# Probabilities transposed in 32x32 squares on VectorE and carried by DMA, in an f32 graph-attention layer

## The reference

```
q, k, v = heads(x @ Wq + bq), heads(x @ Wk + bk), heads(x @ Wv + bv)
scores = einsum('bhqd,bhkd->bhqk', q, k) / sqrt(64)
probs = softmax(scores + where(adj, 0, -9e15)[:, None])
ctx = einsum('bhqk,bhkd->bhqd', probs, v)
out = layernorm(x + merge(ctx) @ Wf + bf)
```

## Time and profile before

| | |
|---|---|
| median of 3 runs | 1510.48 us (1510.31 to 1511.2) |
| the profiled execution | 1509.4 us, its span 1507.4 us |
| PE busy | 1471.1 us, 98% |
| PE's weight loads | 1141.7 us, 76% |
| DVE, ACT, POOL busy | 898.2, 873.4, 378.2 us |
| TensorE's granted clock | 0.997 of full |
| DMA | 51.41 MB, mean 34 GB/s |

### The profile page before, as it was taken

The page is one execution under the profiler, slowest core; times in us unless marked ns, Lnnn a source line. Parts: engine busy times, 40 slices in busy tenths (PEclk is TensorE's granted clock), DMA queues, the critical chain, the costliest instruction groups (busy, mean ns, idle before and its releaser), DMA issues.

```text
span 1507.4 us, 32054 instructions
## 1 busy us (share of the span) xinstructions
PE 1471.1 (98%) x11088; PEld 1141.7 (76%) x11088; DVE 898.2 (60%) x1769; ACT 873.4 (58%) x1637; POOL 378.2 (25%) x676
## 2 busy tenths in 40 slices
PE   7999999999999999999999999999999999999996
PEld 6777787777877778777787777877778777787764
DVE  5666645665556655666555665566655666465654
ACT  4566626666266662666636665366654666546662
POOL 2112242122411224122141221412214122141222
PEclk9999999999999999999999999999999999999998
DMA  3110101100011000100001100011001110000000
GB/s 129 36 40 30 29 27 38 38 29 29 27 50 29 29 29 24 50 30 29 30 24 50 40 29 20 29 49 35 29 19 37 50 29 30 15 25 19 30 22 28
DMA packets 47925, 51.41 MB, mean 34 GB/s; under 512 B 9089, under 2 KB 47745, under 8 KB 47745
## 3 DMA queue, kind: packets, MB, share of 16 engines
q1 hardware_dynamic: 47744, 49.12, 10.5%
HBM read 36.31 MB, written 12.78 MB: 33 GB/s over the span
## 4 chain that ended last, share of the span: by engine, by line
PE 92%; DVE 3%; issue 2%; ACT 1%; POOL 1%; DMA 0%; DVEq 0%; SPq 0%; ACTq 0%; POOLq 0%
PE turn_ps L457 23%; PE context_ps L470 22%; PE score_ps L444 20%; PE misc_ps L356 4%; PE misc_ps L355 4%; PE misc_ps L354 4%; PE score_ps L354 3%; PE score_ps L355 3%; PE score_ps L356 3%; DVE prob L660 1%; PE context_ps L354 1%; PE turn_ps L354 1%; PE context_ps L356 1%; PE context_ps L355 1%; PE misc_ps L362 1%
## 5 line engine op out<-in xcount | busy, mean ns | idle before, releaser
L660 DVE CUSTOM_DVE_ANT_0 prob<-score_ps,mask 128x1024 f32<-128x1024 f32 x384 | 455.0, 1222 | 252.5 <-PE score_ps L444 232.7
L568 ACT ACTIVATE prob_t<-turn_ps 128x512 f32<-128x512 f32 x384 | 229.5, 598 | 431.6 <-PE turn_ps L457 431.6
L559 ACT ACTIVATE prob<-prob,row_min 128x1024 f32<-128x1024 f32 x384 | 442.1, 1151 | 64.3 <-DVE row_min L660 64.3
L457 PE MATMUL turn_ps<-ident,prob 128*128 128x128 f32 x3072 | 413.1, 276 | 9.8 <-ACT prob_t L568 5.5
L457 PEld LDWEIGHTS turn_ps<-ident,prob 128*128 128x128 f32 x3072 | 337.7, 140 | 94.8 <-issue 78.0
L470 PE MATMUL context_ps<-prob_t,v_all 128*64 128x256 f32 x3072 | 372.1, 385 | 0.8 <-ACT prob_t L568 0.8
L470 PEld LDWEIGHTS context_ps<-prob_t,v_all 128*64 128x64 f32 x3072 | 204.6, 136 | 148.9 <-issue 64.0
L806 POOL TENSOR_TENSOR context_lo<-context,context_hi 128x256 fp32r<-128x256 f32 x96 | 70.6, 735 | 938.6 <-ACT context_hi L582 938.6
L669 DVE COPY prob_t<-turn_ps 128x512 f32<-128x512 f32 x192 | 131.7, 686 | 30.7 <-PE turn_ps L457 30.2
L444 PE MATMUL score_ps<-k_hi,q_hi 64*128 64x512 f32 x768 | 140.9, 444 | 4.8 <-issue 3.8
L444 PE MATMUL score_ps<-k_lo,q_hi 64*128 64x512 f32 x768 | 120.4, 390 | 0.0
(11 more groups left out here) (85 smaller groups left out, 1834.9 us busy)
## 6 DMA issues: line engine op xcount, KB each, us to landing
x_in<-in_x_dram SPq DMA_DIRECT2D x32, 384.0 KB, 3.4
inv_rows<-spread_dram SPq DMA_DIRECT2D x192, 64.0 KB, 2.6
out_dram<-res SPq DMA_DIRECT2D x32, 384.0 KB, 2.5
adj_in<-in_adj_dram SPq DMA_DIRECT2D x64, 128.0 KB, 2.2
spread_dram<-inv_turned SPq DMA_DIRECT2D x384, 0.5 KB
prob_t<-in_L_gnn_Wk_dram SPq DMA_DIRECT2D x1, 576.0 KB, 4.3
prob_t<-in_L_gnn_Wq_dram SPq DMA_DIRECT2D x1, 576.0 KB, 7.1
prob_t<-in_L_gnn_Wv_dram SPq DMA_DIRECT2D x1, 576.0 KB, 8.3
```

The source lines that it names most:

```text
L457: last = pe.transpose(turn_ps[:, half, i, :], prob[:, u % 4, kt * P:(kt + 1) * P], ident[:])
L559: nc.scalar.activation(prob[:, t % 4, :], prob[:, t % 4, :], ACT.Exp, scale=-1.0, bias=row_min[:, t % 4:t % 4 + 1], accum_out=row_sum[:, t ...
L568: nc.scalar.activation(prob_t[:, pair % 2, head, 0:4, qt * P:(qt + 1) * P], turn_ps[:, 0], ACT.Copy).then_inc(copied[0], 1)
L660: nc.vector.tensor_tensor_reduce(prob[:, t % 4, :], score_ps[:, t % 2, :], mask[:, qt, :], 1.0, HUGE, ALU.add, ALU.min, row_min[:, t % 4:t ...
```

## The change

PE's transposes, their PSUM tile `turn_ps` and the copies out of it are gone. In their place DVE transposes each 32x32 square of a unit where it stands (`turn_squares`), and sixteen DMAs a slot carry the squares to the partitions of their keys (`move_square`): source partitions 32a to 32a+31, both heads, keys 256c to 256c+255, to the partitions 32c to 32c+31 of `prob_t`. One such DMA has 64 rows of 1 KB. Those with a+c odd are issued from SP's queue, those with a+c even from ACT's. To make a block of 32 partitions hold the keys that it gets, x^T is stored with its tokens permuted (`tokens`).

More changes with it. The layout of inverted row sums is no round trip through DRAM any more: POOL makes a diagonal (`make_diagonal`), and PE multiplies it with ones (job i, 12 a batch). The lo halves of x, k and q are made on POOL from a second copy that ACT makes (`raw`), where DVE made them from PSUM. ACT also copies v out; its bias is folded into the output bias. The whole group is mixed at once (job m), one slot or more after its second slot. `prob` has three slots where it had two. The table `STEADY` says which jobs PE does in which slot; the batch is written out three times (first, the loop of six, last).

```diff
+    9: [("i", 3, 0, 0), ("m", 3, 0, 0)],
+    10: [("x", 0, 0, 1), ("x", 1, 0, 1), ("x", 2, 0, 1), ("q", 0, 2, 0), ("p", 0, 0, 0)],
...
-        prob = sb("prob", [P, 4, S], F32)
-        prob_t = sb("prob_t", [P, 2, 2, TT, GQ], F32)
+        prob = sb("prob", [P, 2 * RING, S], F32)
+        prob_t = sb("prob_t", [P, 2, 2, 2, 4, GQ], F32)
...
+        def move_square(queue, s, a, c):
+
+            group, qt, ring = s // 2, s % 2, s % RING
+            queue.dma_start(prob_t[32 * c:32 * c + 32, group % 2, :, qt, a, :],
+                            prob[32 * a:32 * a + 32, 2 * ring:2 * ring + 2, GQ * c:GQ * c + GQ]
+                            ).then_inc(landed[ring], 16)
...
-                        last = pe.transpose(turn_ps[:, half, i, :], prob[:, u % 4, kt * P:(kt + 1) * P], ident[:])
...
+            def mix(b, group):
+                pe.wait_ge(context_done, at(b, GROUPS, group + 2))
+                for s in (2 * group, 2 * group + 1):
+                    pe.wait_ge(landed[s % RING], at(b, 256 * SLOTS // RING, 256 * (s // RING + 2)))
...
+            def move(b, s):
+                act.wait_ge(squared, at(b, UNITS, 2 * s + 2))
+                if s % 2 == 0:
+                    act.wait_ge(mixed, at(b, GROUPS, s // 2 + 1))
+                for a in range(4):
+                    for c in range(4):
+                        if (a + c) % 2 == 0:
+                            move_square(act, s, a, c)
+
+            def body(b):
+                for s in slots_of(b.mode):
+                    work = slot_work(b.mode, s)
+                    if s < SLOTS:
+                        exponential(b, 2 * s)
+                        exponential(b, 2 * s + 1)
+                    for job in work:
+                        if job[0] not in "pm":
+                            evict(b, job)
+                    if s < SLOTS:
+                        move(b, s)
+                    for job in work:
+                        if job[0] == "m":
+                            context_high(b, job[1])
...
+            def turn_squares(b, t):
+                ring = 2 * (t // 2 % RING) + t % 2
+                dve.wait_ge(exp_done, at(b, UNITS, t + 1))
+                dve.sem_inc(dve_waited, 1)
+                nc.vector.transpose(prob[:, ring, :], prob[:, ring, :]).then_inc(squared, 1)
...
+                    if s < SLOTS:
+                        mask_scores(b, 2 * s)
+                        mask_scores(b, 2 * s + 1)
+                        turn_squares(b, 2 * s)
+                        turn_squares(b, 2 * s + 1)
```

More of the change, by code:

```diff
@@ L72 @@
[L72 to L78, removed]
@@ L81, in mid_job @@
[L81 to L100, removed]
+SLOTS = 24
+RING = 3
+STEADY = {
[24 rows of a table added]
+}
+FIRST_0 = [("k", 1, 0, 0), ("k", 1, 1, 0), ("q", 1, 0, 0)]
@@ new lines, with slot_work @@
+X_LOADS = {1: (0, 0), 2: (0, 1), 3: (0, 2), 4: (0, 3), 11: (1, 0), 12: (1, 1), 13: (1, 2), 14: (1, 3)}
+RESIDUALS = {1: 0, 2: 1, 11: 2, 17: 3}
+NORMALISE = {3: -2, 10: -1, 13: 0, 18: 1}
+START_STEPS = ([("weight", 1)] + [("job", job) for job in START_JOBS[:6]] + [("weight", 0)]
+               + [("job", START_JOBS[6]), ("weight", 2), ("job", START_JOBS[7]), ("weight", 3), ("job", START_JOBS[8])])
+@dataclass(frozen=True)
+class Batch:
+    mode: str
+    it: Any
+    off: int
+def slot_work(mode, s):
+    if s >= SLOTS:
+        return LAST_24 if mode == "last" else []
+    if mode == "first" and s < 2:
+        return FIRST_0 if s == 0 else FIRST_1
+    if mode == "last" and s == 22:
+        return LAST_22
+    return [w for w in STEADY[s] if not (mode == "first" and w[1] < 0) and not (mode == "last" and w[3] == 1)]
@@ L103, in graph_attention, with slots_of @@
+def slots_of(mode):
+    return range(SLOTS + 1 if mode == "last" else SLOTS)
+MODES = ("first", "mid", "last")
+JOBS = {mode: [w for s in slots_of(mode) for w in slot_work(mode, s) if w[0] != "m"] for mode in MODES}
+EVICTED = {mode: [w for w in JOBS[mode] if w[0] != "p"] for mode in MODES}
+SPLITS = {mode: [w for w in EVICTED[mode] if w[0] not in "vi"] for mode in MODES}
 def graph_attention(nc, x, adj, wq, bq, wk, bk, wv, bv, wf, bf, out):
@@ new lines, in _ @@
+            pe.wait_ge(weights_done, 4)
+            pe.wait_ge(bv_wide_done, 1)
+            for t in range(FT):
+                last = pe.matmul(job_ps[:, 0, 0:H], bv_wide[:, t, :], weight_raw[:, 3, t, :],
+                                 start=(t == 0), stop=(t == FT - 1))
+            last.then_inc(bv_mixed, 1)
+            pe.wait_ge(ones_done, 1)
+            body(Batch("first", 0, 0))
+            with pe.Fori(0, len(loop)) as it:
+                body(Batch("mid", it, 1))
+            body(Batch("last", 0, BATCH - 1))
@@ L612, in _, with start_high @@
-            for kind, what in start_steps():
+            def start_high(job):
+                act.wait_ge(job_done, START_JOBS.index(job) + 1)
+                bank = job_bank("start", job)
+                if job[0] == "x":
+                    half = slice(512 * job[2], 512 * job[2] + 512)
+                    nc.scalar.activation(tokens(xt_hi, job[1], half), as_tokens(bank), ACT.Copy).then_inc(hi_done, 1)
+                else:
+                    width, hi, _ = job_parts(job)
+                    bank = bank[:, 0:width]
+                    which = 1 if job[0] == "k" else 0
+                    nc.scalar.activation(hi, bank, ACT.Identity,
+                                         bias=bias_qk[:, which, job[1]:job[1] + 1]).then_inc(hi_done, 1)
@@ L613, in _ @@
+            for kind, what in START_STEPS:
                 if kind == "weight":
```

878 lines of the change are left out of this document (420 added, 458 removed), and 22 rows, old and new, of the table STEADY.

## The result

The changed kernel takes **2015.56 us** (median of 4 runs, 2014.09 to 2016.73); beside it the kernel before took 1510.76 us. The ratio is 1.334, with an interval of 1.332 to 1.336. The forecast was 1676 us, 11% slower. The direction was right and the size was far off: 33% slower, near the upper end of the range. The profiled execution has a span of 2014.0 us and a mean granted clock of 0.834.

The account below looks back on a forecast made before the run. PE bound the kernel before; ACT's issue ring would bound the changed one. 22 to first masking + 5 + 1476 for 191 periods of 7.73 + 143 extras + 26.5 tail = 1673 us span, forecast 1676, range 1490 to 2100.

Parts of the forecast that it names:

- The ring: Each slot pays in turn ACT's eight issues, two exponentials, DVE's second transpose and three handovers: a period of 7.73 us.
- Its part without the issues: Per slot: two exponentials on ACT 2.48 us, the second unit's transpose on DVE 1.22, three handovers 0.2.
- rival 3: DVE's wide transposes take 1.63 us each, about 1790 us in all; at twice the masking's time 2020; chance 12%.
- I take 0.48, the middle of 0.42 and 0.55: 3.84 us.: Price of one DMA issue on ACT, 0.48 us, and of a slot's eight, 3.84 us.
- each 0.1 us of an issue is worth 154 us: Sensitivity of the total time to ACT's issue price; break-even with the kernel before at 0.37 us an issue.
- the upper end of 0.585: Highest price allowed for an ACT issue, 4.7 us a slot, from 256 rows of 1.5 KB at the start.
- Extras of a batch: Beyond 24 periods: context_high 5.4 us, ACT's evictions and slot 4's wait 12.6, output tiles on DVE 1; together 19.
- PE, a slot ahead by then, ends it about 1.5 late: In slot 4 ACT's DMAs wait for slot 5's mix on PE, which ends about 1.5 us late.
- Rival 1: Cheap issues: 0.32 us each on ACT, a period of 6.45 us and a time of 1430 us; chance 15%.
- Rival 2: Both queues take turns making descriptors: period 11.6 us, time 2400 us, or about 2000 with half an issue shared; chance 15%.
- Rival 4: PE's clock falls in idle stretches: 2440 us at 1.2 GHz throughout, some 2000 for half the time; chance 8%.
- 1240 us if PE stayed the bound: Time with PE still the bound after losing its transposes: 149 us a batch, 8 x 149 + 50.

Follow-up runs that it names:

- experiment 2: The changed kernel with ACT's eight squares of a slot left out and prob_t cleared once; SP issues its eight as before: 1410.69 us, ratio 0.934.
- experiment 5: The changed kernel with SP alone issuing, eight transfers a slot, each 128 rows of 1 KB on all 128 partitions, output not the reference's: 1417.24 us.
- experiment 6: The changed kernel with one q job of slot 4 moved behind the mix of slot 5: 1982.53 us, ratio 1.313.
- Experiments 1 and 3: The changed kernel with all sixteen squares on SP's queue: 2284.0 us; and with SP's eight left out, ACT's eight kept: 1973.36 us.
- experiment 7: The changed kernel with four-unit squares, SP issuing twelve and ACT four per two slots, ACT's a slot later; bf16 mask, lo halves on DVE: 1683.25 us.
- experiment 8: The grouped kernel with all sixteen transfers of two slots issued from SP and none from ACT: 1608.58 us, ratio 1.066.
- grouped kernel: The changed kernel with each square carrying four units (128 rows, 128 KB), sixteen issues for two slots; first measured with both queues issuing: 1683.25 us.
- experiment 4: The changed kernel with ACT issuing a slot's squares behind the next slot's exponentials, nothing left out: 1880.31 us, ratio 1.245.
- that last edit: SP-only grouped kernel (1608.58 us): mixes one slot later and other jobs spread, 1412.38 us; mixes alone 1650.11 us, jobs alone 1689.78 us.
- experiment 9: The grouped kernel, SP alone issuing, with mixes one slot later from a batch's third group on and other jobs spread anew: 1412.38 us, ratio 0.936.

## Why the prediction was wrong, step by step

**What held.** PE is busy for 68%, near the 70% forecast, but that is luck: its busy time is 1371 us where 70% of the forecast span is 1171, and both it and the span came out longer. DVE's masking waits 92.8 us for PE and others, not the 252.5 of before. The ring is the one described, as experiment 2 shows by opening it: exponentials behind the issues, transposes behind the exponentials, issues behind the transposes. Its part without the issues was forecast as 2.48 + 1.22 + 0.2 = 3.90 us and is 3.79 in the turn shown (3.80 in the median). The wide transpose, which no row of before showed, takes 1.227 us against 1.22 forecast; rival 3 (slow squares) falls.

**The step that failed** is "I take 0.48, the middle of 0.42 and 0.55: 3.84 us." The issues take 5.56 us a slot in the mean. That is 1.72 us more in each of 192 slots, 330 of the 341 us between the forecast span of 1673 and the span of 2014.0. By "each 0.1 us of an issue is worth 154 us" the start-to-start price of 0.695 (5.56 by eight) would have given 2007. The median issue on ACT (0.619, and 0.65 from start to start) lies above even the upper end of 0.585 that I allowed, and the range held the time only because it had been widened for other rivals. The reasoning behind it was half right: the number of rows hardly sets the price (experiment 5). But I chose between rows of DMAs that have DRAM on one side, 0.32 to 0.585 from start to start, for a transfer from SBUF to SBUF, and took the middle of two of them. The dearest row in sight, the 0.585 of the start, was dismissed as rush; even with it the sum would have been some 1840 us (0.105 x 1540 = 162 more). The mean adds 0.05 to the median: about 0.03 from the 41 issues over 1.0 us and 0.02 from the 138 between 0.7 and 1.0. That an issue is so dear between two places of SBUF is measured; what in it takes the time stays open.

**Extras of a batch.** The middle batches are 246.6 us apart (275.1 to 1754.7, six of them). Less 24 x (3.79 + 5.56) that leaves 22.2, against 19 forecast, but not by the steps given; that the sums lie so close is luck. "PE, a slot ahead by then, ends it about 1.5 late" was wrong: the period there is 17.6 us, some 8 over the usual one. PE isn't ahead: it waits for a bank whose copy stands on ACT (3.4 of the 8, experiment 6), and then does the scores, job i and the mix of slot 5 while ACT waits. The two slots with the evictions of x lose 2.2 and 1.7 us in front of their issues, where 3.2 each was forecast, and the three slots with k at most 0.1, where 1.5 each was. I had no term for the loop's own edge, where ACT shows this after the issues of slot 23 (start us, us, what):

```profile
1011.06 0.05 ACTq L646
1011.11 2.90 issue
1014.01 0.05 ACTq L646
1014.06 0.05 issue
1014.11 0.07 ACT prob L602
```

The five edges of the loop take 2.70 to 3.17 us. The trace of before could have given the term: ACT has the same gap there, 2.47 to 2.72 us at six edges, but with the ring open it lay beside PE's work. In a closed ring it is paid in full.

**The rivals.** Rival 1 (an issue at 0.32) falls by a factor of two. Rival 2 (both queues share what makes the descriptors) gave the right time for the wrong reason, and by luck: its estimate with half an issue shared was about 2000. Experiments 1 and 3 show each queue at the same median price alone. The Trainium skill, "Perfetto Trace Analysis", section "DMA Instruction — HWDGE (DVE, Sync)", has the generator locked for exclusive use and shared by two sequencers; the runs of squares of 64 KB show at most 0.25 us of eight issues that could be such a lock, mostly in one of the eight; with those of 128 KB from both queues there is more (experiment 7). The other rule that was weighed, from the Trainium skill, "DMA: Bandwidth & Descriptors", section "Issuing engines are not separate DMA queues", is that initiating takes usually little beside the DMA itself. This kernel is the other case: an issue takes 0.62 us of the 2.1 from its start to the landing, and on ACT 5.56 us a slot went to initiating half of the transfers. Rival 4: the clock did fall, to 0.834, with PE idle for a third of the time:

```profile
1060.00:1065.00 5.00, 5.00 (x46) 3.06 (x43) 2.38 (x4) 0.00 (x0) 0.00 (x0) 1.00 0.01 3
...
1070.00:1075.00 5.00, 0.00 (x0) 0.00 (x0) 3.29 (x5) 3.37 (x7) 1.14 (x2) 0.50 0.34 90
1075.00:1080.00 5.00, 3.19 (x16) 1.86 (x18) 1.75 (x4) 0.61 (x2) 1.79 (x3) 0.50 0.79 184
```

These are windows (columns as in the earlier trace rows): after a stall the clock is at 0.50, the level of 1.2 GHz, and the next mix runs at it (4.76 us against 3.62). By the chain it costs little here, since PE is 6% of it; no run tested that. It should cost more where PE is nearer the bound, as in the piece of the chain in experiment 8.

**The gain that the change could have had** was there: 1240 us if PE stayed the bound was too low (with ACT free of issues PE is idle for 14 to 15%), but leaving ACT's squares out gave 1411 us, and the grouped kernel in which SP alone issues gave 1412.

## What to carry to other kernels

Count DMA issues as instructions of the engine that issues them, here at about 0.6 us each for 64 or 128 KB from SBUF to SBUF; ask whose order they stand in, and what waits for that engine's next instruction, also for the small copies that end up behind them (experiment 4). Make the transfers fewer and larger, put them on a queue with nothing else to do, and give their consumer the distance that they then need, while each slot's load on the engines stays even: here either half of that last edit alone was slower, and both together were 12% faster. When a new operation's price has to be taken from rows of another kind and the result hangs on it by a factor of eight, take the dearest comparable row for the forecast, not the middle.

## What the runs showed of the hardware

- The median issue from SBUF to SBUF takes 0.60 us on SP and 0.62 on ACT with 64 rows of 1 KB on 32 partitions, and 0.60 to 0.61 and 0.63 with 128 rows on 32; with 128 rows on 128 partitions, one unit each, 0.60, the first of eight 0.47. The median issues of the other repeated transfers (x, mask, residual, output) in the same kernels take 0.34 to 0.43.
- The queues work at the same time. ACT's median price with SP silent is 0.618, with SP issuing 0.619, but in 117 of 192 blocks one of the eight takes 0.7 to 1.0. With squares of 128 KB from both queues (experiment 7) SP's mean goes to 0.725, from 0.638 with ACT silent.
- Every issue of a square over 1.0 us in the changed kernel (41 on ACT, 34 on SP) overlaps in time with one of the 80 packets of 16 KB of the queue for instructions.
- The data of the squares take more time of the 16 DMA engines than the 52 us a MB that I had worked out. In the kernel of experiment 9 it is 0.731 x 16 x 1410.5 / 249.35 = 66 us a MB, in the kernel of experiment 5, with the same number of packets of 1 KB but 128 partitions to a transfer, 0.537 x 16 x 1415.3 / 249.35 = 49. So in the traffic of these two kernels the transfers that touch 32 partitions cost a third more than those across all 128.
- DVE transposes 128x1024 f32 in 32x32 squares in 1.227 us, as fast as it masks them.
- The edge of the loop leaves ACT without work for 2.7 to 3.2 us at five edges (2.5 to 2.7 at six in the kernel before).
